# Last norm of a graph kernel: one-hot rows by VectorE, an identity product, split loads, closer scales

## What is computed

```
x = _layernorm(x + _L1_gnn_ref(x, ...), axis=-1)
# L1:  out = zeros.at[dst].add(msg)
# _layernorm:  (x - mean(x)) / sqrt(var(x) + 1e-5)   over the 32 features
```

## Time and profile before

| | us |
|---|---|
| median of 3 runs | 1983.5 |
| lowest and highest run | 1983.34, 1989.6 |
| span of the profiled execution, first to last instruction | 1707.1 |
| last stage, first register load to last instruction | 1555.8 to 1707.1 |
| mean granted TensorE clock | 0.846 of full |

### The profile page before, as it was taken

The page is one execution under the profiler, slowest core; times in us unless marked ns, Lnnn a source line. Parts: engine busy times, 40 slices in busy tenths (PEclk is TensorE's granted clock), DMA queues, the critical chain, the costliest instruction groups (busy, mean ns, idle before and its releaser), DMA issues.

```text
span 1707.1 us, 25367 instructions
## 1 busy us (share of the span) xinstructions
PE 1315.9 (77%) x6200; PEld 957.6 (56%) x6200; DVE 1193.5 (70%) x3648; ACT 858.9 (50%) x2256; POOL 1068.9 (63%) x1168
## 2 busy tenths in 40 slices
PE   5699993686513777665778999958999999996673
PEld 1388881242212555554655666635777777775563
DVE  9699995677512443676667999964777777774776
ACT  0167770011101222666775777735666666664884
POOL 7777778777777777774111444448877887830444
PEclk8599996577555999888888999977999999997655
DMA  1000000123224988665555666531222222213785
GB/s 41 13 14 13 14 14 20 47 72 79 67 68 127 257 250 246 171 174 145 132 138 140 179 184 189 163 95 32 58 58 57 58 64 67 59 42 78 196 216 157
DMA packets 298498, 178.98 MB, mean 105 GB/s; under 512 B 28715, under 2 KB 290032, under 8 KB 298352
## 3 DMA queue, kind: packets, MB, share of 16 engines
q1 hardware_dynamic: 219712, 116.54, 26.0%
q0 software_dynamic: 29008, 36.18, 8.3%
q10 hardware_dynamic: 49632, 24.65, 5.0%
HBM read 111.18 MB, written 66.07 MB: 104 GB/s over the span
## 4 chain that ended last, share of the span: by engine, by line
PE 42%; POOL 28%; issue 16%; DVE 8%; DMA 2%; DVEq 2%; SPq 1%; ACT 1%; POOLq 0%; ACTq 0%
PE bank L1025 12%; POOL gat L511 12%; POOL lined L518 11%; PE bank L994 7%; PE bank L1018 7%; DVE res L1308 5%; PE bank L945 3%; POOL out L591 3%; PE bank L947 3%; PE bank L1034 3%; PE bank L1003 3%; PE bank L987 3%; DMA placed<-pay,pos_i 1%; DVEq L1308 1%; DVEq L1302 1%
## 5 line engine op out<-in xcount | busy, mean ns | idle before, releaser
L566 POOL DMA_INDIRECT gat<-x_d,src_i x196 | 253.2, 1292 | 59.0 <-issue 53.1
L511 POOL DMA_INDIRECT gat<-in_x,key_i x196 | 211.1, 1077 | 64.8 <-issue 62.4
L1308 DVE TENSOR_TENSOR res<-res,bank 128x128 f32 x588 | 168.4, 286 | 108.5 <-issue 24.4
L528 POOL DMA_INDIRECT placed<-pay,pos_i x196 | 191.9, 979 | 68.1 <-issue 65.6
L518 POOL DMA_INDIRECT lined<-in_x,other_i x196 | 195.8, 999 | 59.7 <-issue 59.7
L1025 PE MATMUL bank<-prod,ident 128*128 128x280 f32 x896 | 217.0, 400 | 0.0
L1025 PEld LDWEIGHTS bank<-prod,ident 128*128 128x128 f32 x896 | 171.0, 191 | 46.5 <-issue 0.6
L956 PE MATMUL bank<-woh,pw 128*128 128x128 f32 x784 | 135.4, 335 | 69.3 <-DVE woh L1287 33.4
L956 PEld LDWEIGHTS bank<-woh,pw 128*128 128x128 f32 x784 | 120.3, 238 | 85.5 <-DVE woh L1287 44.5
L56 ACT ACTIVATE xt<-bank 128x128 f32<-128x128 f32 x98 | 26.6, 271 | 269.6 <-PE bank L897 261.2
L1018 PE MATMUL bank<-rw,ht 65*128 65x384 f32 x392 | 141.3, 514 | 23.3 <-ACT ht L738 13.8
(11 more groups left out here) (204 smaller groups left out, 2840.5 us busy)
## 6 DMA issues: line engine op xcount, KB each, us to landing
pw<-placed SPq DMA_DIRECT2D x588, 68.0 KB, 2.1
pw<-placed SPq DMA_DIRECT2D x98, 272.0 KB
xin<-in_x_t SPq DMA_DIRECT2D x53, 256.0 KB, 3.2
placed<-pay SPq DMA_DIRECT2D x49, 272.0 KB, 2.4
x_d<-res POOLq DMA_DIRECT2D x49, 256.0 KB, 3.8
placed<-pay SPq DMA_DIRECT2D x28, 448.0 KB, 3.2
out<-out ACTq DMA_DIRECT2D x49, 256.0 KB, 2.7
xin<-in_x_t ACTq DMA_DIRECT2D x45, 256.0 KB, 3.6
```

The source lines that it names most:

```text
L511: pool.indirect_dma_start(gat[:, t, :], None, x, bass.IndirectOffsetOnAxis(ap=key_i[:, 0, t:t + 1], axis=0)).then_inc(s_gat, 16)
L528: pool.indirect_dma_start(placed[1].rearrange("t p r -> (t p) r"), bass.IndirectOffsetOnAxis(ap=pos_i[:, 1, t:t + 1], axis=0), pay[i % 4][ ...
L566: pool.indirect_dma_start(gat1[g % 3][:, k, :], None, x1_d, bass.IndirectOffsetOnAxis(ap=src_i[:, t:t + 1], axis=0)).then_inc(c_gat[g % 3] ...
L1308: add.up(dve.tensor_tensor(into, into, quarter(bank + k // G, k % G), ALU.add))
```

## The change

It touches the last stage and nothing else.

- `away_from_4`, its ring `away4` and its semaphore are gone. DVE builds the one-hot rows in one instruction of 128 x 512, comparing the ramp with `kr4`, both broadcast (`hot_4`).
- `add_4` is gone. PE starts each bank with a product of the identity and the batch of `res`, and the four window products accumulate on it. ACT squares out of PSUM and copies the bank back to `res`.
- SP issues three loads of a batch (`BY_SP = 3`), ACT the fourth. Each loads its own tile numbers.
- Roots are taken over groups of 7, 7, 7, 7, 7, 5, 4, 3, 1 and 1 batches. `norm_4` follows `hot_4` by two steps.
- `scale_4` runs up to two batches a step, from the fourth step after the group's last batch. With the group sizes the list `SCALED` holds two, two, two and one batch in four steps and none in the next three. The store of a scaled batch comes one step later, behind that step's squares. `out4` is a ring of four.

```
-            def add_4(b):
-                dve.wait_ge(z_mm, b + 1)
-                done(add)
-                dve.tensor_tensor(batch(b), batch(b), wins(psum[b % 4][:, :]), ALU.add).then_inc(z_y, 1)
+            def hot_4(b):
+                dve.wait_ge(z_kr, b + 1)
+                wait(dve, z_mm, b - 2)
+                dve.tensor_tensor(oh4[b % 3][:, :, :], iota[:, 0:P].unsqueeze(1).broadcast_to([P, G, P]),
+                                  kr4[b % 3][:, :].unsqueeze(2).broadcast_to([P, G, P]), ALU.is_equal).then_inc(z_oh, 1)
...
-            staged([add_4, None, None, norm_4], NB)
+            staged([hot_4, None, norm_4], NB)

# PE
             for b in range(NB):
+                wait(pe, z_y, b - 3)
+                pe.matmul(psum[b % 4][:, :], ident[:, :], flat(b), start=True, stop=False)
                 pe.wait_ge(z_oh, b + 1)
-                wait(pe, z_y, b - 3)
                 for k in range(G):
-                    ins = pe.matmul(quarter(b % 4, k), oh4[b % 3][:, k, :], pw4[b % 6][:, k, 0:P], start=True, stop=True)
+                    ins = pe.matmul(quarter(b % 4, k), oh4[b % 3][:, k, :], pw4[b % 6][:, k, 0:P], start=False, stop=k == G - 1)

# ACT
+            def load_4(b):
+                wait(act, z_mm, b - 5)
+                first_rows(act, mybir.EngineType.Activation, pw4[b % 6], 1, b, range(BY_SP, G), z_pw[b % 6])
+
             def square_4(b):
-                act.wait_ge(z_y, b + 1)
+                act.wait_ge(z_mm, b + 1)
                 wait(act, z_ssq, b - 2)
-                act.activation(wins(sq4[b % 3][:, :]), batch(b), ACT.Square, scale=D ** -0.5).then_inc(z_sq, 1)
+                act.activation(sq4[b % 3][:, :], psum[b % 4][:, :], ACT.Square, scale=D ** -0.5).then_inc(z_sq, 1)
+                act_copy(act, flat(b), psum[b % 4][:, :]).then_inc(z_y, 1)
...
+            act.wait_ge(z_stored, 1)
+            for b in range(5):
+                load_4(b)
+            for s in range(len(SCALED) + STORE_LAG):
+                if s + 5 < NB:
+                    load_4(s + 5)
+                if s < NB:
+                    square_4(s)
+                for b in SCALED[s - STORE_LAG] if s >= STORE_LAG else ():
+                    store_4(b)

# POOL
             def scale_4(b):
-                pool.wait_ge(z_root, b // 4 + 1)
-                wait(pool, z_st[b % 3], 16 * (b // 3))
+                n, o = root_of(b)
+                pool.wait_ge(z_root, n + 1)
+                pool.wait_ge(z_y, b + 1)
+                wait(pool, z_st[b % OUTS], 16 * (b // OUTS))
...
-            staged([apart_4] + [None] * 9 + [scale_4], NB)
+            for s, scaled in enumerate(SCALED):
+                if s < NB:
+                    apart_4(s)
+                for b in scaled:
+                    scale_4(b)
```

More of the change, by code:

```diff
@@ L28 @@
 BURST, LINED = 8, 7
+BY_SP = 3
+ROOTS = [7, 7, 7, 7, 7, 5, 4, 3, 1, 1]
+ROOTED = [sum(ROOTS[:n + 1]) - 1 for n in range(len(ROOTS))]
+SCALE_LAG, STORE_LAG, OUTS = 4, 1, 4
 U = 7
@@ L38 @@
 IN_RANGE = "a prefix sum of counts that add up to the number of rows"
-assert NT == NW and NG * G == NT and NB == NG and 2 * HT == NT and NG % 7 == 0
+assert NT == NW and NG * G == NT and NB == NG and 2 * HT == NT and NG % 7 == 0 and sum(ROOTS) == NB
 assert PAD_NODE + NT * P - E <= NPAD <= OTHER and NPAD * P < 1 << 24
@@ L249, in gnn_kernel @@
         kr4 = ring(sb, "kr4", 3, [P, G])
-        away4 = ring(sb, "away4", 2, [P, G, P])
         oh4 = ring(sb, "oh4", 3, [P, G, P])
         sq4 = ring(sb, "sq4", 3, [P, BC])
[L253 to L257, removed]
+        out4 = ring(sb, "out4", OUTS, [P, BC])
+        ssq4 = ring(sb, "ssq4", 2, [P, max(ROOTS) * G * J])
+        root4 = ring(sb, "root4", 2, [P, max(ROOTS) * G * J])
+        vps4 = sb("vps4", [P, max(ROOTS) * G * J])
+        newt4 = sb("newt4", [P, max(ROOTS) * G * J])
         psum = [ctx.enter_context(nc.psum_tensor(f"bank{n}", [P, 512], F32)) for n in range(8)]
@@ L291, in gnn_kernel @@
         c_prod, c_sum, c_scal, c_pay, c_mm, c_msg = sem("c_prod"), sem("c_sum"), sem("c_scal"), sem("c_pay"), sem("c_mm"), sem("c_msg")
-        z_pw, z_kr, z_away, z_oh, z_mm = ring(sem, "z_pw", 6), sem("z_kr"), sem("z_away"), sem("z_oh"), sem("z_mm")
+        z_pw, z_kr, z_oh, z_mm, z_stored = ring(sem, "z_pw", 6), sem("z_kr"), sem("z_oh"), sem("z_mm"), sem("z_stored")
         z_y, z_sq, z_ssq, z_root, z_out = sem("z_y"), sem("z_sq"), sem("z_ssq"), sem("z_root"), sem("z_out")
-        z_st = ring(sem, "z_st", 3)
+        z_st = ring(sem, "z_st", OUTS)
         S_FIRST, S_EXTRA, D_EXTRA, D_FIRST = (NG * n for n in range(4))
@@ L372, in start_of, with first_rows @@
             return psum[m // 2][0:LO + QT, NW * (m % 2):NW * (m % 2) + NW]
-        def first_rows(sp, to, c, b, landed):
+        def first_rows(eng, on, to, c, b, ks, landed):
             _, tiles = nc.values_load_multi_w_load_instructions(
-                t0_i[0:1, c, G * b:G * b + G], engines=[mybir.EngineType.SP], min_val=0, max_val=NT,
+                t0_i[0:1, c, G * b + ks.start:G * b + ks.stop], engines=[on], min_val=0, max_val=NT,
                 skip_runtime_bounds_check_because=IN_RANGE)
-            for k in range(G):
-                sp.dma_start(to[:, k, :], placed[c][bass.ds(tiles[k], 1)].rearrange("t p r -> p (t r)")).then_inc(landed, 16)
+            for k, tile in zip(ks, tiles):
+                eng.dma_start(to[:, k, :], placed[c][bass.ds(tile, 1)].rearrange("t p r -> p (t r)")).then_inc(landed, 16)
         AHEAD, COUNTS, RANKS = 5, 3, 2
@@ L411, in gnn_kernel, with root_of @@
         BACK = (5, 6, 7)
+        def root_of(b):
+            n = next(n for n in range(len(ROOTS)) if b <= ROOTED[n])
+            return n, G * J * (b - ROOTED[n] + ROOTS[n] - 1)
+        SCALED = []
+        while not SCALED or SCALED[-1].stop < NB:
+            first = SCALED[-1].stop if SCALED else 0
+            ready = [b for b in range(first, min(first + 2, NB)) if ROOTED[root_of(b)[0]] + SCALE_LAG <= len(SCALED)]
+            SCALED.append(range(first, first + len(ready)))
         block = ctx.enter_context(nc.Block())
@@ L446, in _ @@
                 freed(sp, b - 5)
-                first_rows(sp, pw[b % 6], 0, b, s_pw[b % 6])
+                first_rows(sp, mybir.EngineType.SP, pw[b % 6], 0, b, range(G), s_pw[b % 6])
             def load_extra(i, c):
@@ L463, in _ @@
                 wait(sp, s_back, min(i - 5 - D_EXTRA, NG))
-                first_rows(sp, pw[i % 6], 1, b, s_pw[i % 6])
+                first_rows(sp, mybir.EngineType.SP, pw[i % 6], 1, b, range(G), s_pw[i % 6])
                 if b >= 5:
@@ L496, in _ @@
             sp.wait_ge(c_mm, NU)
+            sp.sem_inc(z_stored, 1)
             for b in range(NB):
                 wait(sp, z_mm, b - 5)
-                first_rows(sp, pw4[b % 6], 1, b, z_pw[b % 6])
-            for h in range(3):
-                sp.wait_ge(z_st[h], 16 * len(range(h, NB, 3)))
+                first_rows(sp, mybir.EngineType.SP, pw4[b % 6], 1, b, range(BY_SP), z_pw[b % 6])
+            for h in range(OUTS):
+                sp.wait_ge(z_st[h], 16 * len(range(h, NB, OUTS)))
         @block.gpsimd
@@ L587, in scale_4 @@
             def scale_4(b):
-                pool.wait_ge(z_root, b // 4 + 1)
-                wait(pool, z_st[b % 3], 16 * (b // 3))
-                r = root4[(b // 4) % 2][:, G * J * (b % 4):G * J * (b % 4) + G * J]
-                pool.tensor_tensor(nodes(out4[b % 3][:, :]), rows(b), r.unsqueeze(2).broadcast_to([P, G * J, D]), ALU.mult).then_inc(z_out, 1)
+                n, o = root_of(b)
+                pool.wait_ge(z_root, n + 1)
+                pool.wait_ge(z_y, b + 1)
+                wait(pool, z_st[b % OUTS], 16 * (b // OUTS))
+                pool.tensor_tensor(nodes(out4[b % OUTS][:, :]), rows(b),
+                                   root4[n % 2][:, o:o + G * J].unsqueeze(2).broadcast_to([P, G * J, D]), ALU.mult).then_inc(z_out, 1)
             def apart_4(b):
                 pool.wait_ge(z_pw[b % 6], 16 * G * (b // 6 + 1))
-                wait(pool, z_away, b - 2)
-                pool.tensor_tensor(kr4[b % 3][:, :], w128[:, G * b:G * b + G], pw4[b % 6][:, :, P], ALU.subtract).then_inc(z_kr, 1)
-            staged([apart_4] + [None] * 9 + [scale_4], NB)
+                wait(pool, z_oh, b - 2)
+                pool.tensor_tensor(kr4[b % 3][:, :], pw4[b % 6][:, :, P], w128[:, G * b:G * b + G], ALU.subtract).then_inc(z_kr, 1)
+            for s, scaled in enumerate(SCALED):
[3 more added lines that the diff above has]
+                    scale_4(b)
         @block.scalar
@@ L792, in _ @@
                 sums_3(g)
+            def load_4(b):
+                wait(act, z_mm, b - 5)
+                first_rows(act, mybir.EngineType.Activation, pw4[b % 6], 1, b, range(BY_SP, G), z_pw[b % 6])
             def square_4(b):
-                act.wait_ge(z_y, b + 1)
+                act.wait_ge(z_mm, b + 1)
                 wait(act, z_ssq, b - 2)
```

(26 more changed lines are left out.)

## The result

| | us |
|---|---|
| before, median of 8 runs (seven of 1983.34 to 1989.6, one of 2395.32) | 1986.05 |
| changed, median of 8 runs (1991.43 to 2005.64) | 1997.72 |
| ratio, 95% interval | 1.0065 [1.0049, 1.0081] |

The change makes the kernel slower by 0.65%, some 13 us (the two medians lie 11.7 apart). The forecast was 1996.

A forecast was written before the change was run, and what follows sets the result against it. SP's issuing was taken to bound the last stage. Batches +11.5, clock +6, end -7 and start +2 made +12.5 us, giving a median of 1996 us, range 1967 to 2013.

The forecast's parts named there:

- What bounds the kernel: Last stage before the change: SP's register loads and load issues set the pace, 2.53 us a batch.
- Three words cost more than four: SP's register load: three words taken as 0.65 us against 0.30 for four, making SP's batch 2.23 us.
- The ring: `out4`: a scale waits for the store four batches back to land, stalling 2.7 us in each of six groups.
- The root: `newton` on DVE moves onto the path, the next one-hot rows behind it: 3.5 us over 112 sums.
- A group: Seven batches of the last stage: 16.7 us of turns plus 2.7 of stall, 19.4 us, 2.77 a batch.
- turns: DVE's comparison, POOL's subtraction and scale, and most of `newton` exclude each other on SBUF: 16.7 us a group.
- The second way of making the sum: A group without turns: TensorE's 1.83 us for seven batches, 2.7 of stall, 2.9 of root: 18.4 us.
- The end: Last register load to last store issue: 15 us for 22.3, so -7 us.
- The start: Start of the last stage, TensorE at half clock level with 3.5 us a batch: +2 us.
- The middle: 48 batches at 2.77 for 2.53 us, +11.5, and +6 for TensorE batches at half clock.
- The fast case: Rival: stalls hidden and SP's relief counts, if turns plus stalls stay under 16.5 us a group; 1970 or 1955; chance 0.25.
- The rival of no change: Rival: turns not exclusive and clock full, 2.63 us a batch, total 1983.5; chance 0.14.

The follow-up runs named there:

- all3: Changed kernel with eight places in `out4`, `norm_4` three steps behind `hot_4`, and the comparison's ramp read from a PSUM bank: stage 149.7 us, ratio 0.9996.
- all3_quad: Changed kernel with eight `out4` places, `norm_4` a step later, ramp in a PSUM bank, SP reading four tile numbers: stage 131.2 us, ratio 0.989.
- lag3: Changed kernel with `norm_4` following `hot_4` by three steps for two: stage 159.0 us, ratio 1.0039.
- ring8_quad_lag3: Changed kernel with eight `out4` places, SP reading four tile numbers, `norm_4` three steps behind `hot_4`: stage 138.5 us, ratio 0.9935.

## Why the prediction came out as it did

**Right by its own steps.**

- *What bounds the kernel.* SP's issuing. No run took the issue off SP in the kernel before, so there it rests on the rows: 42 waits of POOL for a load. With the stalls eased it is shown: taking 0.37 us a batch off SP took 18.5 us off the stage (all3 to all3_quad).
- *Three words cost more than four.* 0.65 was taken, 0.67 measured; the reading of DVE's rows, 0.23 a word where no full four is read, comes near on SP as well (3 x 0.23 = 0.69), and one word on ACT is 0.28. SP's batch: 2.23 against 2.25.
- *The ring.* 2.7 us in each of six groups, 16 us. Taking the wait out gave 13.5, of which 12.3 between the first and last subtraction (136.5 to 124.2), 2.05 a group. The mechanism is as the text has it: from the end of TensorE's batch (1866.2) to the subtraction (1871.3) 5.1 us, 5.5 forecast.
- *The root.* 3.5 us over 112 sums; 3.2 from first instruction to the comparison behind it.
- *A group.* 19.4 us, and 0.8 for the clock: 20.2. Measured 19.9.

**Right, for less than the reasons given.** The 19.4 was made of 16.7 of turns and 2.7 of ring. The turns are real, but they don't add: taking them away from the changed kernel gave 1.5 us. The root's stall, which the sum held only as part of the turns, was worth 5.9 when it was eased (lag3). The second way of making the sum (1.83 x 7 + 2.7 + 2.9 = 18.4) names the parts that the experiments confirm, and lacks 1.5 us of the 19.9. That the first came nearer was partly luck. The run ring8_quad_lag3, whose comparison still reads SBUF twice, does a group in about 16.2 us, under the 16.7 that was called a sum of exclusive turns.

**Wrong in size.**

- *The end*, -7, measured -1.3. From the last subtraction to the last store issue the stage took 17.5 before and takes 16.2 now. The step listed batch 47's and 48's roots and left out that the ring holds there too: the scale of batch 44 waits 5.8 us for a store, and the last root waits 3.6 us for the scales behind that one. The wait that the prediction found in the middle it did not carry to the end.
- *The start*, +2 for a TensorE at half level. It is not there: up to the first subtraction the stage takes 0.2 us more, and the first nine steps behind it take 2.0 less, since SP is last in them and had been relieved.
- *The middle*, +11.5 and +6 for the clock, 17.5 together; measured +14.6, the first nine steps included. The granted clock of 0.9 was as foreseen (0.83 over the whole stage). That the price put on its dips was too high, or hidden by the waits, isn't shown by a run.

+12.5 was forecast and +13.6 measured in the stage. The end's error (+6) and those of middle and start (-5) cancel almost fully.

**The rivals.** The fast case decides at turns plus stalls under 16.5 us a group, and they came to 19.9: it came true once stalls were eased and SP read four words (ring8_quad_lag3, all3_quad). The rival of no change was right that the turns cost little, and put a group at 18.4; it had no price for the clock and the same end of -7 as the forecast. POOL keeping its interfaces for two scales: comparisons of 1.59 are the longest, so DVE gets in after one. ACT's loads didn't become last: in each of POOL's waits for a load in the changed kernel, ACT's had landed at least 1.8 us ahead of the last of SP's. Of the signs named, SP waiting for TensorE, the scale waiting for stores and the clock near 0.9 came; a comparison near 1.5 us came 6 times in 49, fewer than "many".

**Outside the trace.** That 276 us lie outside it was false, though harmless for the sum: the change lies behind all of them.

## What to carry to other kernels

When a queue that sets the pace is relieved, look for the waits that were hidden behind it. Here it was a ring: a place comes free when a store has landed, the store is issued behind another wait, and work that comes in bursts of two batches a step uses up four places before the first landing. That cost some 2 us a group of seven. When you make work come in bursts, count the burst and the steps until the landing against the places of the ring, at the end of a stage too. And ease stalls together before judging one alone: here a register load that cost nothing to mend was worth 1 us or 18, by what else stood in the way.

## What the hardware showed beside this

- A register load of four words from a multiple of four is cheaper than one of three from the same place: 0.30 against 0.67 us on SP.
- Beside comparisons with two SBUF inputs POOL's own instruction grew as well, from 1.05 to up to 1.60 us; with one input from a bank it did not (1.12 at most). The rows of before showed only VectorE's side.
- Leaving the identity product out took TensorE's granted clock from 0.83 to 0.67 over the stage, and the stage didn't get shorter (168.2 against 164.9).
- The unchanged kernel takes 1986 to 1995 us in some sets and 1700 to 1705 in others. In the changed kernel's two profiled executions, POOL's gathers of an early stage waited 185 us more for VectorE's index list in the long one, with no such wait in the short one:

```profile
L533 POOL DMA_INDIRECT lined<-in_x,other_i x196 | 196.4, 1002 | 267.0 <-DVE other_i L1258 185.3 <-issue 56.5 <-remote 20.0
```

```profile
L533 POOL DMA_INDIRECT lined<-in_x,other_i x196 | 195.1, 995 | 59.7 <-issue 59.7
```

The cause lies ahead of the last stage and stays open; the ratios aren't touched, since each is made on one chip.
